# A state-space front end on one core: 32-column and 1-column matmuls widened to 64 columns

## The reference, cut to what matters

```python
A_back = I - half * Ac                 # H = N = 64, complex, half = dt / 2
A_fwd = I + half * Ac
dB = dt * solve(A_back, Bc)
dA = solve(A_back, A_fwd)
x = dB[..., None]                      # _krylov(L = 512)
while x.shape[-1] < L:
    x = concatenate([x, A_ @ x], -1)
    A_ = A_ @ A_
k = einsum('chn,hnl->chl', Cc, x).real # C is the image: 32 batches
```

## Time and profile before

| | |
|---|---|
| median of 3 runs | 2889.0 us |
| the profiled execution, its own time | 2887.97 us |
| its span in the trace | 2886.2 us |
| busy: PE, DVE, ACT, POOL | 2453.4, 1936.5, 1405.4, 1215.9 us |
| mean granted TensorE clock | 0.903 of full speed |
| `ssm_kernels` on TensorE | from 13.45 us to 452.9 us |

### The profile page before, as it was taken

The page is one execution under the profiler, slowest core; times in us unless marked ns, Lnnn a source line. Parts: engine busy times, 40 slices in busy tenths (PEclk is TensorE's granted clock), DMA queues, the critical chain, the costliest instruction groups (busy, mean ns, idle before and its releaser), DMA issues. The chain is left out here.

```text
span 2886.2 us, 48591 instructions
## 1 busy us (share of the span) xinstructions
PE 2453.4 (85%) x17080; PEld 2089.8 (72%) x17081; DVE 1936.5 (67%) x2921; ACT 1405.4 (49%) x3474; POOL 1215.9 (42%) x774
## 2 busy tenths in 40 slices
PE   4999997788888888888887782999999579999986
PEld 4999997688887888888887771444444367877775
DVE  7665532999999999999999783222222366777562
ACT  0341335888888888888888430111111123343432
POOL 3200001666666666666666574000000365455331
PEclk9997987999999999999999955999999778999986
DMA  5910000000000000000000073556653221111000
GB/s 191 413 57 1 1 1 30 31 31 32 31 32 31 32 31 32 31 32 31 31 31 31 13 222 107 176 176 238 193 175 124 70 60 44 32 44 32 8 8 16
DMA packets 65440, 209.57 MB, mean 73 GB/s; under 512 B 12224, under 2 KB 17600, under 8 KB 62400
## 3 DMA queue, kind: packets, MB, share of 16 engines
q1 hardware_dynamic: 24832, 95.96, 9.6%
q0 software_dynamic: 28576, 89.16, 9.5%
q10 hardware_dynamic: 11808, 21.50, 2.0%
HBM read 129.96 MB, written 76.62 MB: 72 GB/s over the span
## 5 line engine op out<-in xcount | busy, mean ns | idle before, releaser
L846 POOL TENSOR_TENSOR m_hs<-m_hs,m_BC 128x1040 f32<-128x1040 f32 x256 | 619.0, 2418 | 382.6 <-DVE m_hs L959 382.6
L765 ACT ACTIVATE m_dA<-m_dt,m_A 128x128 f32<-128x128 f32 x2048 | 614.4, 393 | 185.9 <-DVE m_hs L959 111.4
L640 PE MATMUL m_py<-m_hs,ident 128*128 128x130 f32 x4096 | 534.9, 286 | 143.8 <-POOL m_hs L846 143.8
L640 PEld LDWEIGHTS m_py<-m_hs,ident 128*128 128x128 f32 x4096 | 501.8, 199 | 163.4 <-POOL m_hs L846 161.5
L959 DVE TENSOR_TENSOR_SCAN m_hs<-m_dA,m_own 128x1040 f32<-128x1040 f32 x256 | 593.2, 2317 | 35.5 <-ACT m_dA L765 22.7
L944 DVE TENSOR_TENSOR m_own<-m_BC,m_own 128x1040 f32<-128x1040 f32 x256 | 318.7, 1245 | 18.8 <-issue 4.9
L592 PE MATMUL m_pw<-m_xg,m_w_in 128*128 128x130 f32 x2048 | 268.0, 291 | 51.3 <-DVE m_xc L907 34.8
L592 PEld LDWEIGHTS m_pw<-m_xg,m_w_in 128*128 128x128 f32 x2048 | 259.2, 206 | 55.0 <-DVE m_xc L907 37.8
L1444 PE MATMUL e_pG<-ew_gu,e_xT 128*128 x656 | 236.2, 504 | 11.0 <-issue 7.4
L1424 POOL DMA_DIRECT2D e_x<-regions x80 | 42.9, 536 | 404.9 <-PE e_pX L1435 404.9
L1444 PEld LDWEIGHTS e_pG<-ew_gu,e_xT 128*128 128x128 f32 x656 | 120.0, 193 | 91.9 <-issue 26.1
(11 more groups left out here) (290 smaller groups left out, 4453.9 us busy)
## 6 DMA issues: line engine op xcount, KB each, us to landing
m_BC<-xs SPq DMA_DIRECT2D x16, 2080.0 KB, 9.9
slots<-a_zero POOLq DMA_DIRECT2D x48, 512.0 KB, 44.9
ew_gu<-in_gate_up_w SPq DMA_DIRECT2D x32, 768.0 KB, 5.0
e_x<-regions POOLq DMA_DIRECT2D x82, 256.0 KB, 3.0
slots<-e_y ACTq DMA_DIRECT2D x82, 256.0 KB, 2.6
regions<-a_zero POOLq DMA_DIRECT2D x16, 512.0 KB, 15.6
ew_d<-in_down_w SPq DMA_DIRECT2D x32, 256.0 KB, 5.6
out_h<-t_ho SPq DMA_DIRECT2D x8, 520.0 KB, 3.3
```

The lines of the kernel that those rows point to most:

```text
L640: mm = pe.matmul(py[k % 2][:, 0:MT], ident[:, :], hs[u % NB][:, n, :], start=False, stop=(half == 1 and n == HN - 1))
L765: act.activation(images(dA[u % NB][:, n, :])[:, :, 1:TOK], images(dt[b][:, k, :])[:, :, 1:TOK], ACT.Exp, scale=A[:, at:at + 1]).then_inc(d ...
L846: pool.tensor_tensor(hs[u % NB][:, :, :], hs[u % NB][:, :, :], BC[b][:, ST + half * HN:ST + (half + 1) * HN, :], ALU.mult).then_inc(prod_r ...
```

## The change

The constant TWICE = 2 is new. `row` now reads its 32 columns twice (a moving operand of 2 times 32 columns, with step 0 over the 2) and writes 64 columns a head, so 512 columns, the whole first bank of the unit. `first_column` reads its single column 64 times over and writes columns 64 to 127 of each head. VectorE's copy of a row (L407 before, L409 after) takes the first 32 of each 64 columns; nobody reads the others. The numbers and the order of the instructions, the weights, the semaphores and their values are the same on every engine.

```diff
+TWICE = 2
...
             def first_column(g, u):
                 pe.wait_ge(h_ready, after_round(g + 1, u, 2))
                 for h in range(u * NH, (u + 1) * NH):
-                    mm = pe.matmul(out(u)[:, h % NH, HN:HN + 1], V[:, h, :], U[:, h, HN:HN + 1], start=True, stop=True)
+                    mm = pe.matmul(out(u)[:, h % NH, HN:P], V[:, h, :], U[:, h, HN:HN + 1].broadcast_to([P, P - HN]), start=True, stop=True)
...
                 for h in range(u * NH, (u + 1) * NH):
-                    mm = pe.matmul(bank[u][:, 0, h % NH * BATCH:(h % NH + 1) * BATCH], V[:, h, :], L[:, h, j - 1, :], start=True, stop=True)
+                    mm = pe.matmul(bank[u][:, 0, h % NH * TWICE * BATCH:(h % NH + 1) * TWICE * BATCH].rearrange("p (s c) -> p s c", s=TWICE),
+                                   V[:, h, :], L[:, h, j - 1, :].unsqueeze(1).broadcast_to([P, TWICE, BATCH]), start=True, stop=True)
...
                         dve.wait_ge(mm_done, after_round(g * MMS + MMS - FT + j, u))
-                        dve.tensor_copy(L[:, hs(u), j, :], bank[u][:, 0, 0:NH * BATCH].rearrange("p (h c) -> p h c", h=NH)).then_inc(l_ready, 1)
+                        dve.tensor_copy(L[:, hs(u), j, :], bank[u][:, 0, :].rearrange("p (h s c) -> p h s c", h=NH, s=TWICE)[:, :, 0, :]).then_inc(l_ready, 1)
```

## The result

The changed kernel takes 2850.24 us (median of 4 runs, 2849.22 to 2851.02), the kernel before 2888.63 us in the same comparison (4 runs, 2883.84 to 2889.16). The ratio is 0.9872, with a 95% interval of 0.986 to 0.9884: 1.3% or 38.4 us faster, clear of the scatter of the runs. The forecast was 2849, with a range of 2838 to 2860.

The account below looks back on a forecast made before the run. TensorE, busy in the front end, was taken to be bound by a clock that narrow products halve. Savings of 15.6 us in group 0 and 24.7 in group 1, 40.3 in total, gave 2849 us, range 2838 to 2860.

Parts of the forecast that it names:

- L160 and L165: First-column product and transposes behind it, at full clock: 4.6 + 2.0 us saved in group 0, 4.5 + 2.05 in group 1.
- Rows 1 and 2 of group 0, and L134: Rows j = 1 and 2 at full clock save 2.0 and 6.4 us; the four L134 instructions save 0.4 us.
- The gap: TensorE's wait between rows j = 2 and 3 of group 0: VectorE's time, 3.6 us stay, 0.2 us saved.
- Row 3: Row j = 3 of group 0: clock falls in the wait before it, 64 columns hold it low, 13.86 us, 0 saved.
- L225 of group 0: Last product of group 0: recovers the clock within itself as now, 9.20 us, 0 saved.
- Group 1: Nothing stands between its rows: L184's 192 instructions save 16.8 us, L225 starts at full clock and saves 1.35 us.
- Costs at nothing: Additional columns are covered by the weight load, 113 ns an instruction with repeated reads; VectorE's copy stays at 0.42 us.
- 64 columns hold the level that they find: Rule read off TensorE's rows: 64-column products keep the clock at whichever level they find, high or low.
- row 3 at full clock: Rival: row j = 3 of group 0 takes 6.6 us less and L225 1.9 us less; 2840 us, chance 0.17.
- A clock held for a while only: Rival: 64 columns lose the clock after some 7 us, saving only 6 us; 2883 us, chance 0.08.
- nothing happens to the clock: Rival: the low clock comes from something other than narrow products; 2889 us, chance 0.04.
- slow repeated reads: Rival: step-0 reads set the pace, 228 ns for each of 512 L160 and L184 instructions; 2901 us, chance 0.05.

Follow-up runs that it names:

- column_only: The kernel before with only the first column read 64 times and the rows left at 32 columns; 2875.0 us, ratio 0.9959 to the kernel before.
- no_gap: The changed kernel with `prepare` step 3 and `spread` reordered to remove the wait before row j = 3 of group 0; 2837.5 us, ratio 0.9833 to before.
- j3_wide: The changed kernel with row j = 3 of group 0 reading its 32 columns four times, 128 columns; 2841.2 us, ratio 0.9845 to the kernel before.
- residual_wide: The changed kernel with the first residual reading its 64 columns twice, 128 columns; 2842.1 us, ratio 0.9845 to the kernel before.
- after_again: The changed kernel run once more, unaltered, on another chip; 2863.1 us, where the kernel before took 2909.8 us, ratio 0.9847.
- rows_only: The changed kernel with the first column read once again, so only the rows are widened to 64 columns; 2859.3 us, ratio 0.9909 to the kernel before.
- all_three: The changed kernel with the order without the gap, and the first residual and row j = 3 of group 0 at 128 columns; 2853.5 us, ratio 0.98 to before.
- rows_longer: The changed kernel with 128 extra 64-column instructions behind the rows of group 1, their output unread; 2884.7 us, ratio 0.9924 to the kernel before.
- no_gap_narrow: The kernel before, with 32 and 1 columns, in the order that removes the wait before row j = 3; 2887.0 us, ratio 0.9995 to the kernel before.
- both_added: The changed kernel with the order without the gap and the first residual at 128 columns; 2834.5 us, ratio 0.9816 to the kernel before.
- spread_wide: The changed kernel with the order without the gap and `spread` reading its 16 columns eight times, 128 columns; 2860.8 us, ratio 0.9836 to before.

## Why the prediction was right

The mark moved by 38.6 us where the steps added up to 40.3, and the missing 1.7 us are the last product of group 0 (1.0) and small things: a first step 0.1 us later and Newton rounds of 58.70 us where 58.47 stood. That the time came out within 1.2 us of the forecast is partly luck, since the rest of the program moves it by several microseconds from one execution to the next; that the saving at the mark came out within 1.7 us of the sum is not.

- **L160 and L165.** Forecast 4.6 + 2.0 and 4.5 + 2.05 us; measured 4.54 + 1.96 and 4.45 + 2.05 (7.31 and 3.66 us in both groups). column_only shows that these belong to the column alone.
- **Rows 1 and 2 of group 0, and L134.** Forecast 2.0 + 6.4 + 0.4, measured 2.03 + 6.44 + 0.44.
- **The gap.** Forecast 3.6 us left, measured 3.59 (211.69 to 215.28). That figure was right for the changed kernel and was read wrongly for the experiments: it held 1.3 us of work.
- **Row 3.** Forecast 13.86 us, measured 13.88. This was the step with most risk in it, and both of its halves were shown apart: the clock falls right behind the gap, and with the gap gone three quarters of the row have the full clock (no_gap). The other half is that 64 columns do not bring it back (j3_wide, residual_wide).
- **L225 of group 0.** Forecast no change, measured 10.23 us against 9.20, 1.0 us dearer. This is the one term that was off. In after_again, the same code, it took 8.82, and over all runs a last product that began at the low clock took from 8.61 us (before, group 1) to 10.33 (rows_only, group 0). "Recovers within itself as now" holds only to within that.
- **Group 1.** Forecast 16.8 + 1.35 us for L184 and L225, measured 16.68 + 1.25.
- **Costs at nothing.** Reading 32 columns twice or one column 64 times costs nothing that counts: 113 ns an instruction for the rows, as for the 64-column products that read no column twice, and 114 ns (7.31 us) for the single column. VectorE's copy of 32 in 64 columns stayed at 0.42 us.
- **What paces an instruction.** The prediction calls the weight load "the obvious thing" and shows no row for it. The trace of the kernel before bears it out: at full clock, products of 65 columns take 113 ns each with weights of 128 columns and 53 ns with weights of 65 (the second has 32 rows instead of 128):

```profile
335.53 7.26 PE L175 MATMUL a_bank<-a_U,a_V 128*128 128x65 f32 x64
2595.09 1.71 PE L1818 MATMUL t_pS<-t_qk 32*65 32x65 f32 x32
```

  The transposes have it the other way round, weights of 64 columns and 128 columns streamed, and take 114 ns (3.66 us for 32). So 128 streamed columns take about as long as the load of 128 columns of weights, and the cover ends between 128 and 260 columns (228 ns).
- **The slices.** The prediction reads dips of the clock in the second, fifth, sixth and seventh slices. The row prints them in the fourth, sixth and seventh (7, 8 and 7); the second and the fifth have 9, as the slices without a dip do. The account was built on the timeline, so nothing else rests on this.

Of the rivals, row 3 at full clock is what all_three makes of it, not what the change did. A clock held for a while only is refuted by rows_longer over 35.7 us; that nothing happens to the clock, by the windows of the changed kernel at 1.00; slow repeated reads, by the pace. The rule of the Trainium skill (TensorE: Matmul & The Clock Gate, "The two states you'll see") that the low level follows idleness agrees with the gap, in which TensorE is busy for 1.41 of 3.50 us, but not with the rest: no_gap_narrow has TensorE busy without a wait through its 32-column rows and runs them at the low pace.

The reading "64 columns hold the level that they find" needs one correction. It is right for a stretch of nothing else, as far as it was tried (35.7 us up, 13.9 us down). With the 16-row `spread` steps among them, 64 columns lost the clock with TensorE busy all the time (no_gap, both_added, spread_wide), and 128 columns did not (all_three).

## What to carry to other kernels

Where TensorE is busy without a break and its instructions suddenly take twice as long, look at how many columns they stream, beside the granted clock: a product whose pace does not depend on its columns (here up to 128, in 32-bit floats) can be widened for nothing, by reading the same columns again into PSUM that nobody reads. Look at the step behind a wait in particular, since a width that holds the high clock (64 here) need not be the one that brings it back (128 here). And when a gap is removed by order, subtract the work that stood in it before putting a price on it.

## What was not expected of the hardware

- Two widths act differently on the clock: at 64 columns products stayed at 1.00 for 35.7 us when they found it there, and at the low pace for 13.9 us when they found that, twice over (the first residual and row 3).
- Making the `spread` products 128 columns wide did not keep the clock up; making the rows around them 128 wide did.
- The rest of the program, the same code in every kernel here, took 2426.8 to 2434.9 us from the mark to the end in the profiled executions of the first nine kernels of the table. The differences lie mainly in the last stage (attention and linear, from its first product into t_pR), which took 624.8 us before, 627.6 in the changed kernel and 620.3 in no_gap. A difference of a few microseconds in the medians here is therefore no evidence; for that the mark is needed, and below some 1.5 us (414.3 against 412.9 for the same code) only the steps themselves tell.
